# Output blocks of a two-layer graph network: products issued by term over all jobs of a step, each term behind its own wait

## The reference, cut to what matters

```python
attn = agg.reshape(n, D) @ Wo[l].T + bo[l]
x = _batchnorm(x + attn, g1[l], beta1[l])
ff = jax.nn.relu(x @ W1[l].T + b1[l]) @ W2[l].T + b2[l]
x = _batchnorm(x + ff, g2[l], beta2[l])
```

## Time and profile before

| | us |
|---|---|
| median of 3 runs | 1103.1 |
| lowest and highest | 1102.02, 1103.13 |
| the profiled execution | 1102.37 |
| its span, first to last instruction | 1100.6 |
| TensorE busy, matmuls | 1024.3 |
| VectorE busy | 764.3 |
| ScalarE busy | 597.7 |
| GpSimd busy | 305.0 |

### The profile page before, as it was taken

The page is one execution under the profiler, slowest core; times in us unless marked ns, Lnnn a source line. Parts: engine busy times, 40 slices in busy tenths (PEclk is TensorE's granted clock), DMA queues, the critical chain, the costliest instruction groups (busy, mean ns, idle before and its releaser), DMA issues. The chain is left out here.

```text
span 1100.6 us, 18765 instructions
## 1 busy us (share of the span) xinstructions
PE 1024.3 (93%) x6579; PEld 852.9 (77%) x6579; DVE 764.3 (69%) x2350; ACT 597.7 (54%) x1096; POOL 305.0 (28%) x312
## 2 busy tenths in 40 slices
PE   4899899998999999999899999899999999989853
PEld 3677677787888888887799889788888888869842
DVE  6767656567777777777488720677777777747787
ACT  6642322446666666666335532566666666652366
POOL 1000000005444444443032100344444444421304
PEclk9899999999999999999999999999999999999985
DMA  6042410568512122113203346441211211320403
GB/s 147 24 159 79 118 45 25 114 159 188 113 38 62 39 47 53 39 34 107 106 1 123 95 115 131 123 94 38 62 38 39 62 38 39 113 87 1 95 3 94
DMA packets 50758, 84.98 MB, mean 77 GB/s; under 512 B 15230, under 2 KB 33506, under 8 KB 50412
## 3 DMA queue, kind: packets, MB, share of 16 engines
q1 hardware_dynamic: 50668, 83.82, 30.7%
HBM read 36.50 MB, written 21.61 MB: 53 GB/s over the span
## 5 line engine op out<-in xcount | busy, mean ns | idle before, releaser
L1274 POOL TENSOR_SCALAR probs<-probs,mass_inv 125x1250 f32<-125x1250 f32 x160 | 211.1, 1319 | 343.1 <-DVE mass_inv L1401 343.1
L1392 DVE CUSTOM_DVE_ANT_0 probs<-banks,scores_bias 125x416 f32<-125x416 f32 (+1 forms) x480 | 267.2, 582 | 45.9 <-PE banks L1294 41.5
L1294 PE MATMUL banks<-k_stack,q_stack 128*125 128x416 f32 (+1 forms) x960 | 294.6, 392 | 2.1 <-DVEq L1379 2.1
L1308 PE MATMUL banks<-ident,probs 125*125 125x125 f32 x1600 | 258.6, 276 | 8.1 <-DVE probs_t L1383 5.9
L1308 PEld LDWEIGHTS banks<-ident,probs 125*125 125x125 f32 x1600 | 240.4, 187 | 32.0 <-issue 22.3
L1362 ACT ACTIVATE probs<-probs,neg_peak 125x1250 f32<-125x1250 f32 x160 | 213.4, 1334 | 54.4 <-DVE neg_peak L1415 54.4
L1349 ACT ACTIVATE probs_t<-banks 125x500 f32<-125x500 f32 x320 | 152.6, 478 | 107.7 <-PE banks L1308 107.7
L1323 PE MATMUL banks<-probs_t,v_pair 125*64 125x250 f32 x1600 | 186.2, 379 | 0.9 <-ACT probs_t L1349 0.9
L1294 PEld LDWEIGHTS banks<-k_stack,q_stack 128*125 128x125 f32 x960 | 143.8, 188 | 30.4 <-issue 16.3
L1323 PEld LDWEIGHTS banks<-probs_t,v_pair 125*64 125x64 f32 x1600 | 107.5, 136 | 54.2 <-ACT probs_t L1349 1.3
L1383 DVE COPY probs_t<-banks 125x500 f32<-125x500 f32 x160 | 108.1, 676 | 54.5 <-PE banks L1308 54.5
(11 more groups left out here) (256 smaller groups left out, 1409.3 us busy)
## 6 DMA issues: line engine op xcount, KB each, us to landing
q_stack<-q_split SPq DMA_DIRECT2D x160, 125.0 KB, 2.3
scores_bias<-edge_bias SPq DMA_DIRECT2D x8, 1171.9 KB
edge_bias<-bias_row SPq DMA_DIRECT2D x10, 585.9 KB
k_stack<-k_lo SPq DMA_DIRECT2D x16, 312.5 KB, 4.4
resid<-residual SPq DMA_DIRECT2D x2, 2500.0 KB, 9.8
values<-v_stage SPq DMA_DIRECT2D x2, 1680.0 KB
residual<-t SPq DMA_DIRECT2D x4, 625.0 KB, 3.0
xs<-in_x SPq DMA_DIRECT2D x5, 480.0 KB
```

The source lines that it names most:

```text
L1274: nc.gpsimd.tensor_scalar(probs[:, u % 4, :], probs[:, u % 4, :], mass_inv[:, u % 4:u % 4 + 1], 1.0, ALU.mult, ALU.mult).then_inc(att["pro ...
L1294: mm = nc.tensor.matmul(pb[0:NT, t % 5, 0:sn], q_stack[:, n % 2, half, part, tile * NT:(tile + 1) * NT], k_stack[:, head * N + s0:head * N ...
L1308: mm = nc.tensor.transpose(pb[0:NT, 5 + t % 2, j * NT:(j + 1) * NT], probs[:, u % 4, (j0 + j) * NT:(j0 + j + 1) * NT], ident[0:NT, 0:NT])
L1392: nc.vector.tensor_tensor_reduce(out=probs[:, slot % 4, s0:s0 + sn], in0=pb[0:NT, t % 5, 0:sn], in1=scores_bias[:, (n % GROUPS) * GROUP + ...
```

## The change

In a step k the three terms become three passes. For a wave, `steps` lists (k, term) pairs, and each pass issues one matmul for every job of the wave before the next term begins. "o" takes the terms as HH, HL, LH, "f" and the K wave as HH, LH, HL. "g" takes HH and LH of both k first and HL of both k last. The waits are split by term: HH asks for the high part alone (for "o" also for the weight's high part), HL for the low part of the features, LH of "o" for the weight's low part. In "f" and the K wave the HH and HL waits stand ahead of each job's matmul, and for the last k they ask a job of chunk 0 only for the first half of the block. Each job's wait for its bank stays where it was, at its first matmul, which is now in the first pass.

```diff
--- before.py
+++ after.py
@@ -1561,31 +1561,46 @@
                             continue
                         hi, lo, whi, wlo, depth = {"o": (a_hi, a_lo, wo_hi, wo_lo, DC), "f": (h1_hi, h1_lo, w1_hi, w1_lo, DC),
                                                    "g": (r_hi, r_lo, w2_hi, w2_lo, FC)}[kind]
-                        for k in range(depth):
-
-                            if kind == "o":
+                        HH, LH, HL = (whi, hi), (wlo, hi), (whi, lo)
+                        if kind == "g":
+                            steps = [(k, term) for terms in ((HH, LH), (HL,)) for k in range(depth) for term in terms]
+                        else:
+                            steps = [(k, term) for k in range(depth) for term in ((HH, HL, LH) if kind == "o" else (HH, LH, HL))]
+                        for s, (k, term) in enumerate(steps):
+                            if kind == "o" and term is HH:
+                                pe.wait_ge(oph["a_hi"], k + 1)
+                                pe.wait_ge(oph["hi"], k + 1)
+                            elif kind == "o" and term is HL:
                                 pe.wait_ge(oph["a_lo"], k + 1)
+                            elif kind == "o":
                                 pe.wait_ge(oph["done"], k + 1)
-                            elif kind == "f":
-                                pe.wait_ge(oph["h1_lo" if k < DC - 1 else "h1_lo_last"], k + 1 if k < DC - 1 else 2)
+                            elif kind == "f" and s == 0:
                                 pe.wait_ge(oph["done"], first_turned[-1] + 1)
+                            elif kind == "g" and (k, term) == (0, HL):
+                                for i in range(FC):
+                                    pe.wait_ge(oph[f"r_lo{i}"], wave[0][2] + 1)
                             for t, (_, c, n) in enumerate(wave, first):
-                                if k == 0 and t >= 8:
+                                if s == 0 and t >= 8:
                                     if ojobs[t - 8][0] == "g":
                                         pe.wait_ge(oph["g_done"], t - 7 - g_first)
                                     else:
                                         pe.wait_ge(oph["done"], t - 7)
                                 s0, sn = CHUNKS[n]
-                                if kind == "g" and k == 0:
+                                if kind == "g" and s == 0:
 
                                     for i, h in enumerate((h1_hi, h1_lo)):
                                         nc.tensor.matmul(pb[:, t % 8, 0:sn], ident_r[:, :], h[:, c, s0:s0 + sn], start=i == 0, stop=False)
-                                    for i in range(FC):
-                                        pe.wait_ge(oph[f"r_lo{i}"], wave[0][2] + 1)
-                                for s, (w, h) in enumerate(((whi, hi), (wlo, hi), (whi, lo))):
-                                    mm = nc.tensor.matmul(pb[:, t % 8, 0:sn], w[:, k, c * P:(c + 1) * P], h[:, k, s0:s0 + sn],
-                                                          start=kind != "g" and k + s == 0, stop=k == depth - 1 and s == 2)
-                                if k == depth - 1:
+                                    pe.wait_ge(oph["r_hi"], FC * (wave[0][2] + 1))
+                                if kind == "f" and term is HH:
+                                    pe.wait_ge(oph["h1_hi"], k + 1 if k < DC - 1 or n == 0 else DC + 1)
+                                if kind == "f" and term is HL and k < DC - 1:
+                                    pe.wait_ge(oph["h1_lo"], k + 1)
+                                if kind == "f" and term is HL and k == DC - 1:
+                                    pe.wait_ge(oph["h1_lo_last"], 1 if n == 0 else 2)
+                                w, h = term
+                                mm = nc.tensor.matmul(pb[:, t % 8, 0:sn], w[:, k, c * P:(c + 1) * P], h[:, k, s0:s0 + sn],
+                                                      start=kind != "g" and s == 0, stop=s == len(steps) - 1)
+                                if s == len(steps) - 1:
                                     mm.then_inc(oph["filled"], 1)
 
                     if last_layer:
@@ -1596,17 +1611,22 @@
                     r = RING_OF[1]["wk"]
                     pe.wait_ge(oph["done"], turned_at[-1] + 1)
                     for k in range(DC):
-                        pe.wait_ge(oph["h_lo" if k < DC - 1 else "h_lo_last"], k + 1 if k < DC - 1 else 2)
-                        for t in range(K_WAVE):
-                            if k == 0:
-                                pe.wait_ge(oph["g_done"], len(ojobs) - 8 + t + 1 - g_first)
-                            _, c, n = JOBS[1][t]
-                            s0, sn = CHUNKS[n]
-                            for s, (w, h) in enumerate(((wt_hi[r], h_hi), (wt_lo[r], h_hi), (wt_hi[r], h_lo))):
+                        for s, (w, h) in enumerate(((wt_hi[r], h_hi), (wt_lo[r], h_hi), (wt_hi[r], h_lo))):
+                            for t in range(K_WAVE):
+                                if k + s == 0:
+                                    pe.wait_ge(oph["g_done"], len(ojobs) - 8 + t + 1 - g_first)
+                                _, c, n = JOBS[1][t]
+                                if s == 0:
+                                    pe.wait_ge(oph["h_hi"], k + 1 if k < DC - 1 or n == 0 else DC + 1)
+                                elif s == 2 and k < DC - 1:
+                                    pe.wait_ge(oph["h_lo"], k + 1)
+                                elif s == 2:
+                                    pe.wait_ge(oph["h_lo_last"], 1 if n == 0 else 2)
+                                s0, sn = CHUNKS[n]
                                 mm = nc.tensor.matmul(pb[:, bank_of(1, t), 0:sn], w[:, k, c * P:(c + 1) * P], h[:, k, s0:s0 + sn],
                                                       start=k + s == 0, stop=k == DC - 1 and s == 2)
-                            if k == DC - 1:
-                                mm.then_inc(proj["filled"], 1)
+                                if k == DC - 1 and s == 2:
+                                    mm.then_inc(proj["filled"], 1)
                     for t in range(K_WAVE, len(JOBS[1])):
                         project(pe, 1, t)
                     bank_freed(pe, 1, former(1, len(JOBS[1])))
```

## The result

| | us |
|---|---|
| after, median of 5 runs | 1111.49 |
| lowest and highest | 1110.07, 1113.24 |
| before, beside it, median of 5 runs | 1102.70 (1101.92 to 1103.13) |
| after / before | 1.0081, 95% interval 1.0067 to 1.0095 |
| the profiled execution of after | 1111.49, span 1109.7 |

A forecast was written before the change was run, and what follows sets the result against it. TensorE, busy 93% of the span, bounds the kernel, with VectorE's chain a hidden second bound. Layer 0's 2.4, the K hand-over's 2.8 and layer 1's 2.4 make 7.6 us later: 1110.7 us, range 1106.5 to 1113.5.

The forecast's parts named there:

- 1: First "o" wave, layer 0: sixth product waits for its bank until 538.96; TensorE ends the wave 1.0 us later.
- 2: VectorE behind the "o" wave: first copy 2.9 us later; after its hole it goes on at 556.8, 1.7 us late.
- 3: "f" wave: a 1.7 us bank stall replaces 1.8 of stalls; wave ends 1.3 us later, r_hi 3.2 later.
- 4: "g" jobs: POOL's last r_lo ends at 590.4; everything behind is 2.4 us later.
- 5: K wave, layer 0: 1.5 us bank stall, wave end within 0.2; first k_stack copy and ninth job 2.8 us later.
- layer 1: Layer 1's output blocks repeat layer 0's; everything behind them 2.4 us later.
- The clock rival: K hand-over: the clock partly falls to 1.2 GHz, 1.7 us lost, 1112.4 us; chance 0.06.
- Step 6: TensorE's queue: some 278 more waits, taken as costing nothing; upper bound 2.8 us in all.
- The faster rival: "f" and K waves: high products fill the waits and nothing else ends later, 5.1 us gained, 1098.0; chance 0.07.
- The two rivals by which VectorE or the hand-over would have hidden the lag: VectorE makes up its lag, K hand-over hidden: 1104.5, chance 0.08; only the K hand-over hidden: 1107.9, chance 0.10.
- The bound on waits (0.01 us each): Rival on TensorE's queue: added waits cost their bound, 2.8 us in all, 1113.5 us; chance 0.04.
- the estimate of 3.7 us: K wave and "o" jobs: 208 repeated weights at 0.018 us would save 3.7 us; not taken into the sum.

The follow-up runs named there:

- fill: As w_once, plus twelve unused matmuls between the transposes and the first product of each first "o" wave; 1108.97 us, +7.4 over before.
- w_once: The changed kernel, same product order, but each wait already covered by an earlier wait of the same wave left out; 1112.85 us, +11.3 over before.
- o_jobs: As w_once, but the first "o" wave goes job by job again; 1106.42 us, +4.9 over before.
- all_jobs: Kernel before with the change's split waits: every wave job by job, only an "o" job takes HL ahead of LH; 1098.66 us, -3.1 against before.
- mixed: As w_once, but "o" job by job, "f" and K waves in passes only at the middle steps, "g" as changed; 1095.75 us, -6.0 against before.
- k_jobs: As w_once, but the K wave goes job by job again; 1107.40 us, +5.8 over before.
- f_jobs: As w_once, but the "f" wave goes job by job, waits by term; 1108.26 us, +6.4 over before.
- o_last_jobs: As w_once, but only the last step (k = 3) of the first "o" wave goes job by job; 1110.45 us, +8.6 over before.
- o_first_jobs: As w_once, but only the first step (k = 0) of the first "o" wave goes job by job; 1107.36 us, +5.5 over before.
- early_only: As all_jobs, with "g" as changed and chunk 0 of the first "o" wave's first four jobs issued by term; 1097.61 us, -4.2 against before.

## Why the prediction was right

**Sign, size and mechanism held.** The forecast was 7.6 us on top of before; it measured 8.8, and 7.4 where no clock fall disturbs (fill). Point by point, with 0.18 taken off the times of after:

| step | forecast | trace of after |
|---|---|---|
| 1, sixth "o" product released by wo_lo | 538.96 | 538.89 |
| 1, "o" wave ends (TensorE's next work starts 551.97) | 551.89 | 551.79 |
| 2, VectorE's first sum | 2.9 later | 2.9 later (551.12) |
| 2, VectorE's reciprocal | 556.8 | 556.77 |
| 3, "f" stall on the sum of job 17, until | 570.25 | 570.11 |
| 3, r_hi | 3.2 later | 3.0 later |
| 4, end of the last r_lo (589.30+1.08) | 590.4 | 590.2 |
| 5, K stall on ScalarE's copy | 1.5 | 1.32 |
| 5, first k_stack copy | 5.2 later | 4.9 later |
| 5, ninth K job | 5.2 later | 4.9 later |
| layer 1 | 2.4 | 4.0 |

Layer 0's terms were right to 0.3 us, most of them a little too large, in part by the pace, below, and in part by the lag behind a wait: the sixth "o" product starts 0.06 us after its wo_lo ends (538.33+0.68=539.01 and 539.07), where the prediction had 0.13. **The term that was off is layer 1's**, 1.6 us too small: it was taken as a copy of layer 0, and in that execution the clock fell behind the stall. fill, where it does not fall, has 118.55-116.08=2.5 us, against the forecast's 2.4.

**The clock rival** had its mechanism right and its place incomplete. It was put in the K hand-over alone, with 1.7 us. That stretch does show the fall, though not in after's execution: 0.57 at 630 to 635 us in w_once, 0.50 at 625 to 630 in o_jobs. The other place, the first "o" wave, was not thought of at all, though the earlier trace rows has the same pattern, transposes and then an idle stretch. What the falls cost a median is known only roughly: w_once lies 3.9 us above fill, with three falls in its profiled execution; of after I have one execution, with one fall and 1.5 us.

**Step 6, waits,** held in its own words: a wait that is met costs nothing that these runs can tell. But the change was priced only as a whole. The prediction names the high products that no longer wait as an effect of their own and gives them no sum; all_jobs shows that the net of 7.4 us is a gain of 3.1 and a loss of 10.5.

**The faster rival**, 1098.0, failed for the reason given, banks and VectorE's chain. Its condition (nothing else ends later) can be met by another order, though: mixed does, at 1095.75. The two rivals by which VectorE or the hand-over would have hidden the lag are refuted by the rows at 570.29 and 630.64. The bound on waits (0.01 us each) would have made fill, without 92 of them in layer 0, 0.9 us shorter than after from T to layer 1; it is 0.06 longer. The other 148 of the 278 were not taken out by themselves.

**Repeated weights.** The sum held without a gain from them. In after the first "o" wave puts 66 products between 539.37 and 551.97, 0.1909 us each, and the K wave 80 between 607.80 and 623.03, 0.1904; the "f" wave, whose passes have no two products running with the same block, puts 66 between 570.59 and 583.13, 0.1900. The kernel before has 0.1906 in that "o" wave (71 between 537.28 and 550.81) and 0.1903 in its "f" wave (35 between 566.29 and 572.95). So the pace of 0.1918, read from the single "o" jobs, was a little too long for the other waves, in either kernel, and the repeats gave nothing that can be seen. The Trainium skill, TensorE: Matmul & The Clock Gate, Part 2, says that separate loading "lets you load once and matmul repeatedly"; the estimate of 3.7 us went by that. This trace shows no such gain, with one weight load recorded for each of 6579 matmuls. The estimate was also too high by its own rule: counted in the programs, the new order has 204 repeats, but the kernel before has 52 already, which leaves 152x0.018=2.7 us.

## What to carry to other kernels

Split a coarse wait first and keep the order: one or two products ahead of each low part took 3.1 us off here, while reordering the same products cost 10.5. On an in-order queue, issuing by term over all jobs asks for every bank at once and ends every job at once; look in the trace for who reads banks out, ahead of the wave and behind it, before doing it, and use passes only in the middle steps, where neither a bank is taken nor a job ends. Where a stall replaces another one of the same length, compare what each stands behind: here one after five products, instead of before the first, came with a fall of the clock in some executions.

## What the runs showed of the hardware

I had not expected that the granted clock could depend on where a stall of 1.5 us lies. Where TensorE had done the sixteen transposes and then only five products, with a stall of 0.52 us ahead of the fifth and one of 1.51 behind it, the clock fell in the next stretch in some executions and not in others: in after in layer 1 (0.66) and not in layer 0 (1.00 in 535 to 545), in w_once in both, in k_jobs, f_jobs and o_last_jobs in layer 1 (0.66 each). In the seven kernels whose "o" wave begins job by job or interleaved, and in fill, no such stretch has less than 1.00, and neither has the kernel before, which idles 1.53 us in one piece between the transposes and its first product. The second place is the hand-over of the K wave, where sixteen transposes come in four groups with idle time between. It has under 1.00 in w_once, o_jobs, f_jobs and o_last_jobs, all with that wave in full passes (but 1.00 in after, fill and o_first_jobs, which have them too), and never where it is job by job or has passes only in the middle. In o_jobs:

```profile
620.00:625.00 5.00, 2.83 (x16) 2.00 (x15) 3.80 (x7) 4.84 (x10) 0.00 (x0) 0.94 0.00 0
625.00:630.00 5.00, 4.78 (x16) 3.87 (x16) 3.63 (x7) 4.87 (x11) 0.00 (x0) 0.50 0.66 155
630.00:635.00 5.00, 5.00 (x25) 4.89 (x24) 4.88 (x10) 2.60 (x6) 0.00 (x0) 0.88 0.43 104
```

In 625 to 630 sixteen matmuls, transposes among them, stand where a full stretch has 28 products at 2.4 GHz. These falls may also widen the spread of runs (3.6 us in w_once and 5.2 in o_last_jobs, but 1.6 in fill), but they are not all of it: mixed, which has none of them, spreads over 4.1 us. Its profiled execution was the slowest of its five runs, 4 us above the others, and seems to have lost that ahead of T, where nothing was changed: T lies at 536.51 us against 532.43 in early_only, and the clock falls there in 35 to 45, 50 to 60 and 120 to 135 us, for example

```profile
125.00:130.00 5.00, 5.00 (x16) 2.90 (x15) 0.61 (x2) 0.00 (x0) 0.00 (x0) 0.50 0.79 248
```

The distances from T leave this out; the medians do not. Each kernel has only one profiled execution, so how often the clock falls is not shown, nor where it falls in the unprofiled runs. Whether a filler in the K hand-over would gain was not tried.
